# One cast and one low of 2048 columns for a step of four products, in place of two of each of 1024

## The reference

```python
def _L0_rec_ref(x, W_enc, b_enc, W_dec, b_dec):
    B, L, D, F = (1024, 2, 1024, 4096)
    f = jax.nn.relu(jnp.einsum('bld,ldf->bf', x, W_enc) + b_enc)
    x_hat = jnp.einsum('bf,lfd->bld', f, W_dec) + b_dec
    return x_hat
```

## Time and profile before

| | |
|---|---|
| median of 3 runs | 655.7 us (655.62 to 656.09) |
| profiled execution | 656.08 us, span in the trace 654.3 us |
| PE busy | 643.9 us, 98% |
| DVE busy | 562.0 us, 86% |
| ACT busy | 339.9 us, 52% |
| POOL busy | 27.7 us, 4% |
| 512 KB load of `w_raw`, issue to landing, median | 4.2 us (decoder), 4.3 us (encoder) |
| granted TensorE clock | 0.999 of full speed |

### The profile page before, as it was taken

One profiled execution on the slowest core, in us unless ns is written; L12 is line 12 of the kernel. 1 busy time (PEld: TensorE's weight loads), 2 busy tenths in 40 slices (PEclk: granted clock), 3 DMA queues, 4 the chain that ended last, 5 costly groups with the idle time before them and its releaser, 6 DMA issues.

```text
span 654.3 us, 8053 instructions
## 1 busy us (share of the span) xinstructions
PE 643.9 (98%) x2904; PEld 526.3 (80%) x2904; DVE 562.0 (86%) x736; ACT 339.9 (52%) x427; POOL 27.7 (4%) x38
## 2 busy tenths in 40 slices
PE   9989999999999999999999999999999999999997
PEld 6778888888887788888888888788877888888886
DVE  4799999879979956669897599999999999998854
ACT  5655445335465445455655657544555445464452
POOL 0110200001100000000000000001100011011000
PEclk9999999999999999999999999999999999999999
DMA  8966896567845554655445465469945589589625
GB/s 320 394 187 226 247 280 238 198 180 224 240 155 169 186 198 145 204 182 173 166 145 195 163 242 191 174 228 241 276 176 189 194 243 263 204 214 314 205 100 192
DMA packets 45206, 138.43 MB, mean 212 GB/s; under 512 B 5296, under 2 KB 6064, under 8 KB 45168
## 3 DMA queue, kind: packets, MB, share of 16 engines
q1 hardware_dynamic: 40176, 124.04, 54.0%
q0 software_dynamic: 4416, 13.37, 10.9%
q10 hardware_dynamic: 576, 0.52, 0.2%
HBM read 120.61 MB, written 4.19 MB: 191 GB/s over the span
## 4 chain that ended last, share of the span: by engine, by line
PE 77%; DVE 13%; DMA 3%; issue 3%; SPq 2%; ACT 1%; DVEq 0%; ACTq 0%
PE sums L696 25%; PE sums L698 25%; PE sums L697 25%; DVE w_split L486 5%; PE sums L753 3%; DVE w_raw L486 3%; DMA w_raw<-w_enc 2%; DVE forms L486 2%; DVE s_sum L486 2%; DVE place L486 1%; DMA w_raw<-w_raw 1%; SPq L244 1%; SPq L237 0%; ACT w_split L348 0%; SPq L238 0%
## 5 line engine op out<-in xcount | busy, mean ns | idle before, releaser
L348 ACT CAST w_split<-w_raw 128x1024 fp32r<-128x1024 f32 (+1 forms) x251 | 236.1, 947 | 269.3 <-PE sums L698 199.5
L696 PE MATMUL sums<-w_split,forms 128*128 128x512 f32 x900 | 355.1, 395 | 4.8 <-DVE w_split L486 3.2
L698 PE MATMUL sums<-w_split,forms 128*128 128x512 f32 x900 | 350.9, 390 | 0.0
L697 PE MATMUL sums<-w_split,forms 128*128 128x512 f32 x900 | 350.5, 389 | 0.0
L486 DVE TENSOR_TENSOR w_split<-w_raw,w_split 128x512 fp32r<-128x512 f32 (+1 forms) x253 | 265.2, 1085 | 60.9 <-ACT w_split L348 59.9
L696 PEld LDWEIGHTS sums<-w_split,forms 128*128 128x128 f32 x900 | 169.0, 188 | 45.4 <-issue 9.4
L698 PEld LDWEIGHTS sums<-w_split,forms 128*128 128x128 f32 x900 | 168.9, 188 | 36.1
L697 PEld LDWEIGHTS sums<-w_split,forms 128*128 128x128 f32 x900 | 169.1, 188 | 33.7
L486 DVE TENSOR_TENSOR w_raw<-w_raw 128x512 f32<-128x512 f32 x238 | 163.8, 688 | 8.1 <-DMA w_raw<-w_dec 2.7
L486 DVE TENSOR_TENSOR forms<-place,forms 128x512 fp32r<-128x512 f32 (+2 forms) x51 | 29.1, 570 | 7.7 <-ACT forms L366 3.3
L486 DVE TENSOR_TENSOR place<-place,sums 128x1024 f32<-128x1024 f32 (+1 forms) x26 | 29.5, 1175 | 5.9 <-PE sums L698 3.7
(11 more groups left out here) (26 smaller groups left out, 79.5 us busy)
## 6 DMA issues: line engine op xcount, KB each, us to landing
w_raw<-w_dec SPq DMA_DIRECT2D x96, 512.0 KB, 4.2
w_raw<-w_enc SPq DMA_DIRECT2D x93, 512.0 KB, 4.3
place<-place POOLq DMA_DIRECT2D x20, 512.0 KB, 8.0
w_raw<-w_enc SPq DMA_DIRECT2D x32, 256.0 KB, 2.7
w_raw<-w_dec SPq DMA_DIRECT2D x32, 256.0 KB, 2.8
place<-xT SPq DMA_DIRECT2D x8, 512.0 KB, 10.7
outT<-place SPq DMA_DIRECT2D x12, 256.0 KB, 2.1
w_raw<-w_raw POOLq DMA_DIRECT2D x10, 256.0 KB, 4.7
```

The costliest lines, as they stand in the source:

```text
L348: nc.scalar.copy(split(s, q, 0), w_pos(s, 2 * q, n)).then_inc(hi_done, 1)
L696: nc.tensor.matmul(out[:, m, :], v_hi, w_hi[:, cols], start=start, stop=False)
L697: nc.tensor.matmul(out[:, m, :], v_lo, w_hi[:, cols], start=False, stop=False)
L698: last = nc.tensor.matmul(out[:, m, :], v_hi, w_lo[:, cols], start=False, stop=stop)
```

## The change

In the steps of four products from the third chunk on (`whole_step`: 16 to 31 and 78 to 109, 48 steps) the two casts of 1024 columns become one of 2048, and the two low parts become one. `hi(s, 0)` and `lo(s, 0)` return at once; the work is done where `hi(s, 1)` and `lo(s, 1)` stood, with the waits of the second half, and each adds 2 to its semaphore. The waits of PE and SP stay as they are.

```diff
--- before.py
+++ after.py
@@ -201,6 +201,16 @@
         def split(s, q, part):
             n = 2 if q == 0 or FOUR[s] else 1
             return w_split[:, s % 2, q, part, 0:n * C]
+
+        def whole_step(s):
+
+            return FOUR[s] and s >= 2 * PAIRS
+
+        def split_whole(s, part):
+            return w_split[:, s % 2, :, part, :]
+
+        def raw_whole(s):
+            return w_pos(s, 0, 4).rearrange("p (q f) -> p q f", q=2)
 
         def banks(p):
             return sums[:, 2 * p:2 * p + 2, :]
@@ -337,6 +347,8 @@
         @block.scalar
         def _(act):
             def hi(s, q):
+                if whole_step(s) and q == 0:
+                    return
                 act.wait_ge(w_loaded[s % RAW], 32 * (s // RAW + 1))
                 if s in T1_DMA:
                     act.wait_ge(w_summed[s % RAW], t1_count(s))
@@ -344,6 +356,9 @@
                     act.wait_ge(w_sums_done, W_SUMS[s + 1])
                 if s >= 2:
                     act.wait_ge(multiplied, BLOCKS[s - 2][q])
+                if whole_step(s):
+                    nc.scalar.copy(split_whole(s, 0), raw_whole(s)).then_inc(hi_done, 2)
+                    return
                 n = 2 if q == 0 or FOUR[s] else 1
                 nc.scalar.copy(split(s, q, 0), w_pos(s, 2 * q, n)).then_inc(hi_done, 1)
 
@@ -504,6 +519,12 @@
                 add(w_pos(s, 2), w_pos(s, 2), w_pos(s, 3)).then_inc(w_sums_done, 1)
 
             def lo(s, q):
+                if whole_step(s):
+                    if q == 1:
+                        dve.wait_ge(hi_done, 2 * s + 2)
+                        add(split_whole(s, 1), raw_whole(s), split_whole(s, 0).bitcast(F32),
+                            ALU.subtract).then_inc(lo_done, 2)
+                    return
                 dve.wait_ge(hi_done, 2 * s + q + 1)
                 n = 2 if q == 0 or FOUR[s] else 1
                 add(split(s, q, 1), w_pos(s, 2 * q, n), split(s, q, 0).bitcast(F32),
```

## The result

The changed kernel takes 661.57 us (661.23 to 661.81), the kernel before 655.66 us (655.27 to 656.09) beside it: a ratio of 1.0087, 95% interval 1.0075 to 1.0099. It is slower by 5.9 us; 661.0 was forecast, with a range of 658.2 to 664.5. The profiled execution took 661.75 us with a span of 659.9, 5.6 more than before.

What follows compares the result with a forecast made beforehand. PE's matmul stream sets the time, fed by how far split weights are ahead, with VectorE nearly full. Losses 0.4 + 0.8 + 1.6 + 3.1 + 1.9 = 7.8 us in place of 2.5: +5.3, giving 661.0 us, range 658.2 to 664.5.

Steps and rivals of the forecast that it cites:

- The size of the instructions: In the 48 merged steps: one cast of 2048 columns takes 1.92 us, one `lo` of 2048 about 2.29 us.
- (a): Steps 17 and 18: `take_out` instructions and sums around the later `lo` make step 18 late, 0.4 us lost.
- (b): Steps 25 and 26: GpSimd's DMA addition lands about 1.9 us later, so `lo` 26 is late; 0.8 us lost.
- rival 3: Between steps 26 and 31 the loop of load, GpSimd's addition and `lo` has no room: 663 to 666 us; chance 0.11.
- the other steps up to 31 stay below 0: Steps up to 31 other than 18 and 26: `lo` comes in time, so PE loses nothing there.
- (c): Step 78, first of the dec2 chunks, loses 0.85 us by a late `lo`; with steps 79 to 83 together 1.6.
- (d): Steps 86 to 99: `lo` 87 waits for its cast, 0.98 us lost, then 2.1 in steps 89 to 99; together 3.1.
- (e): Steps 102 to 108: the same late entry, 1.24 us at step 104 and 0.67 at 107; together 1.9.
- `copy_out` wait: Third product of step 78: PE loses 0.3 us to a late third `copy_out`; it starts 0.95 earlier, so this loss goes.
- Hidden anyway: Whole kernel: VectorE runs ahead through the bursts as before and nothing changes, 655.7 us; chance 0.06.
- Faster: Steps 88 to 99 and 78 to 83: VectorE's saving of 0.06 a step counts, 1.4 us with `copy_out`: 654.3; chance 0.04.
- The raw ring closes: Steps 26 to 31: bunched transfers cost 0.5 to 1 us a turn; with decoder loads 2 to 5 on top; chance 0.11.

Runs made afterwards that it cites:

- one low: Against the kernel before: two casts of 1024 with the waits of before, one `lo` of 2048 in the 48 steps; 658.57 us, ratio 1.0043.
- halves at the entries: The changed kernel, but steps 17, 18, 25, 26, 29, 78, 79, 87, 88, 103 and 104 by halves as before; 658.66 us, 1.0046 against the kernel before.
- the late gate: The kernel before, casts and lows still 1024, but in the 48 steps the first cast also waits for all products of step s-2; 658.33 us, 1.0040.
- three relieved steps: The changed kernel with the first sum of steps 93, 94 and 96 moved from VectorE to GpSimd's accumulating DMA; 661.78 us, 1.0094 against the kernel before.
- 14 relieved steps: First sum of steps 79 to 83 and 91 to 99 moved from VectorE to GpSimd's DMA: in the kernel before 665.34 us, in the changed one 673.99 us.
- seven quiet steps: The change in steps 19, 20, 21, 85, 86, 101 and 102 alone, the others as in the kernel before; 655.87 us, 1.0004.
- one cast: The changed kernel with `lo` taken back: one cast of 2048, two lows of 1024 in the 48 steps; 661.9 us, 1.0096 against the kernel before.

## Why the prediction was right

**The size of the instructions** was right to 0.01 us each. **The deadline rule** (end of `lo` + 0.22 against the due start) held as well: PE started 0.15 us after the end of the `lo` it had waited for at each of these steps but 78 (0.26). The waits measured in the changed kernel, refilling included, against the forecast: step 18 0.46 (0.4), 26 0.79 (0.8), 78 1.13 (0.85), 81 0.57 (0.65), 88 1.03 (0.98), 91, 94 and 97 0.60, 0.62 and 0.60 (0.65 each), 104 1.30 (1.24), 107 0.63 (0.67).

**(a) and (b)**: right in place and size. The timeline from step 25 to 29:

```profile
153.17 2.29 DVE L501 TENSOR_TENSOR w_split<-w_raw,w_split 128x2048 fp32r<-128x2048 f32 x1 [0.31 <-ACT w_split L360]
...
160.04 2.29 DVE L501 TENSOR_TENSOR w_split<-w_raw,w_split 128x2048 fp32r<-128x2048 f32 x1
...
162.47 0.47 PE L717 MATMUL sums<-w_split,forms 128*128 128x512 f32 x1 [0.56 <-DVE w_split L501]
...
169.34 1.42 DVE L501 TENSOR_TENSOR w_raw<-w_raw 128x512 f32<-128x512 f32 x2 [1.48 <-DMA w_raw<-w_raw]
```

`lo` 26 ends at 160.04 + 2.29 = 162.33. That is 60.92 after the start of step 15 (101.41), 0.46 of it the wait before step 18; without it 60.46, where the prediction had 162.33 - 101.91 = 60.42. That the absolute number is the same is chance, and the path was not quite that of (b): the addition of step 26 was 0.4 us earlier than worked out, and `lo` 25 then waited 0.31 us for its cast. So the late cast set this place, as it does in (a), and not the addition; the two dates lay so close that the size came out the same. What (b) missed is step 29: VectorE waited 1.48 us for GpSimd's addition before 169.34, and PE lost 0.33. That is rival 3 at small scale. Issues and landings from 140 to 185 us (KB each, median us):

```profile
w_raw<-w_raw POOLq DMA_DIRECT2D x6, 256.0 KB, 6.2
```

It was 4.6 us before. The runs with one low and with halves at the entries have one such wait too (0.54 before step 29, 0.62 before step 28); the late gate, whose lows end earlier, has none. How much the changed kernel pays differs between executions, and two more traces show it, since their kernels (three and 14 relieved steps) are the changed one up to step 78. With three relieved steps, in the changed kernel and with 14, VectorE waited 0.41, 1.48 and 2.71 us for the addition of step 29, and the steps 15 to 30 lost 1.27, 1.69 and 2.61 us. Only the first is what (a) and (b) forecast (1.2). The median landing was 5.5, 6.2 and 5.4 us, so the one addition decides, and why it is late in one execution and not in another the traces don't tell. Such additions made the trials with 14 steps fail as well. So "the other steps up to 31 stay below 0" was wrong, by 0.3 us in the profiled execution and by up to 1.3 in another.

**(c)** was short by 0.28 us:

```profile
397.59 1.91 ACT L360 CAST w_split<-w_raw 128x2048 fp32r<-128x2048 f32 x1 [2.71 <-PE sums L719]
...
399.61 2.29 DVE L501 TENSOR_TENSOR w_split<-w_raw,w_split 128x2048 fp32r<-128x2048 f32 x1
```

The cast of step 78 started 0.57 after the first matmul of step 77 (397.02) and not 0.27, so that `lo` started 2.59 after it where it was 2.42 before: 0.17 of the 0.28. The other 0.11 is that PE started 0.26 after the end of this `lo`. The trace names the reason of neither. **(d) and (e)** were right: 3.05 for 3.1 and 1.99 for 1.9. The removal of the `copy_out` wait inside step 78 came as worked out.

**The sum**: 8.5 lost against 7.8 forecast, less 2.5 before, less the 0.5 us shorter start-up, which isn't part of the change. That the profiled execution came within 0.3 us of the forecast's 5.3 in span is in part luck: the two misses above (0.3 each, both too low) were nearly offset by the start-up. The medians differ by 5.9.

**The rivals.** *Hidden anyway* fell: only in steps with nothing else to do on VectorE can no cost be seen (seven quiet steps, 1.0004). *Faster* fell. VectorE is the bound for about ten steps, and 0.06 us a step is saved, but the late gate alone makes it begin the sums in front of them 1.3 us later. The Trainium skill ("Perfetto Trace Analysis", Optimizing Scalar/DVE Operations) has both rules. The runs agree with its second one, that breaking up the instructions of an engine that isn't saturated but causes bubbles elsewhere may complete work sooner: by halves the kernel takes 655.66 us, whole 661.57. Its first, that grouping can improve throughput on a saturated engine, brought nothing here, though VectorE is busy 94 to 95% of the time in three of the windows. *The raw ring closes* was real in the encoder, at 0.3 us in the profiled execution and up to 1.3 in another. That rival's second part, late loads in the decoder, didn't come: over the whole span VectorE's sums waited 2.9 us for loads of `w_dec`, and 2.7 before.

**Which part of the change costs** was not in the prediction, and the runs tell it. The gate alone costs 2.8 us, one low alone 3.1, one cast (with its gate) 6.4, all of it 5.9. They don't add, because each moves the end of the same `lo`, and the order of `take_out` against `lo` decides whether VectorE's idle time can be used.

## What to carry to other kernels

Merging two halves saves one fixed cost (0.06 us here) and moves two dates: the start waits for the later of the two inputs, and the consumer of the first half waits for the end of both. Work out the cushion that is left in a steady step (here 0.7 us of 5.44), and then the largest burst of other work on the same engine; if the burst is larger, each one is paid, even where the engine's busy time falls. What an in-order engine has behind the later instruction (here the `take_out` that frees a PSUM bank) belongs to the price.

## What the runs showed of the hardware that was not expected

In the kernel before with 14 relieved steps, PE stood 7.2 us in one piece. Busy time in windows, the seventh figure is the granted clock:

```profile
460.00:468.00 8.00, 6.72 (x30) 5.24 (x28) 1.83 (x3) 2.09 (x3) 2.60 (x3) 1.00 1.03 223
468.00:474.00 6.00, 0.29 (x1) 0.32 (x2) 2.96 (x4) 2.45 (x3) 0.86 (x1) 0.76 0.88 204
474.00:480.00 6.00, 6.00 (x19) 4.75 (x19) 5.83 (x9) 1.83 (x3) 0.00 (x0) 0.67 0.64 188
480.00:486.00 6.00, 6.00 (x29) 4.95 (x27) 5.93 (x9) 2.11 (x2) 0.86 (x1) 1.00 0.76 191
```

The clock was at 1.00, fell in the window of the wait, and was 0.67 over the 6 us behind it, though PE was busy all the time. The timeline above has neighbouring matmuls at 475.13 and 475.56, 0.43 us apart in place of 0.227, the lower of the two levels of 1.2 and 2.4 GHz. From 478.0 on they were 0.23 apart again. So this wait cost its own length and about 2 us more. The changed kernel with the same edit repeats it: PE stood 7.9 us before 479.70, the granted clock was 0.57 from 479 to 486 us, with starts again 0.43 apart, and 1.00 from 486 on. The waits of 1.3 us and less in the changed kernel left the clock at 1.00 in all four windows.
